# Cross-attention kernel: input tiles turned by VectorE's block transposition instead of TensorE, with layer norm statistics gathered through DRAM

## The chip, the cores and the metric

The kernel runs on one core of a Trainium2 chip (trn2). The metric is the device time of one execution in microseconds (us). Runs of the unchanged kernel lie between 3229.87 and 3229.97 us, with a median of 3229.92 us.

## The reference, cut to what matters

```python
# x: (32, 512, 512) queries, ctx: (32, 512, 512) keys and values; 16 heads of 32
def layer_norm(x, gamma, beta, eps=1e-05):
    mu = jnp.mean(x, axis=-1, keepdims=True)
    var = jnp.var(x, axis=-1, keepdims=True)
    return (x - mu) * jax.lax.rsqrt(var + eps) * gamma + beta

qn = layer_norm(q, q_norm_g, q_norm_b)
kvn = layer_norm(kv, kv_norm_g, kv_norm_b)
Q = (qn @ Wq).reshape(B, N_q, NUM_HEADS, D_HEAD).transpose(0, 2, 1, 3)
K = (kvn @ Wk).reshape(B, N_kv, NUM_HEADS, D_HEAD).transpose(0, 2, 1, 3)
V = (kvn @ Wv).reshape(B, N_kv, NUM_HEADS, D_HEAD).transpose(0, 2, 1, 3)
scores = jnp.einsum('bhqd,bhkd->bhqk', Q, K) / jnp.sqrt(jnp.float32(D_HEAD))
attn = jax.nn.softmax(scores, axis=-1)
ctx = jnp.einsum('bhqk,bhkd->bhqd', attn, V)
ctx = ctx.transpose(0, 2, 1, 3).reshape(B, N_q, D_ATTN)
out = q + jax.nn.gelu(ctx @ Wo + bo, approximate=False)
```

Everything is float32. The kernel splits each factor of a product into a high and a low part and adds three products of them.

## The kernel before, in words

The kernel goes through 32 batches. A batch has 512 query tokens and 512 context tokens of 512 features, held as eight tiles of 128 tokens (`tok`, tiles 0 to 3 from x and 4 to 7 from the context). The attention of a batch has four units of four heads; the loop body `batch(b)` has four steps, one for each unit.

The instruction streams of the five engines are written out by hand in the table `ORDER`: a string for each engine and step, whose words are the items of work, in the order in which the engine issues them (`s*4` is four items `s`). `items` turns the strings into a plan, and the code of each engine is one loop over its plan with an `if` for each kind. Each engine waits only through semaphores. What the items are:

- PE (TensorE): `st` is one matmul of transposed scores (L888), 16 in a step, which ACT turns into exponentials. `s` is one matmul of scores (L896), 16 in a step, from which DVE takes a maximum; it is for the unit of the next step. `st` and `s` share four PSUM banks in rotation. `q`, `k`, `v` and `o` are sixths of a projection, two matmuls each (L868). `pv` is one half of the product with V (L916), `z` the sums of rows (L859), `m` turns the maxima (L978; it ends a step). `x` turns one input tile: four transposing matmuls of 128x128 (L956).
- ACT (ScalarE): `st` the exponential (L575), `norm` applies the layer norm to a tile in place (L596), `x` takes the high part of a turned tile out of PSUM (L600), `mh` and `mx` write the maxima into `q_stack` (L625, L629), `gelu` (L592), and `q`, `k`, `v`, `split` copies.
- DVE (VectorE): `s` the maximum over a bank (L718), `ln` the statistics of a tile (`bn_stats`, L737), `la` their aggregation (`bn_aggr`, L743), `lv` variance plus epsilon and negated mean (L748, L749), `x` the low part of a turned tile (L694), `zt`, `zr`, `zb`, `cn` the normalization of the output (L723 to L734), `md` and `ml` for the maxima (L777, L783), `ob` the bias.
- POOL (GpSimd): `add` (L487), `ln` the power -1/2 and the negated shift of one tile (L503, L506), `res_add`, `split`.
- SP (SyncE) issues DMAs, all into one queue and in the order of its string: `load` an input tile (L398), `rq` and `rk` three DMAs each that restack the rows of q and k for the scores (L357), `rz` zero rows (L422), `store` and `res` the output and the residual (L441, L406). `rq`, `rk` and `rz` of a step serve the `s` items of the next one.

The projections, `v`, `o` and the turned tiles `x` share three PSUM banks `gen`. Their rotation is worked out from the order of PE's plan (`GEN`, `GEN_AT`, L161 to L171): before it writes a bank, an engine waits until the item three places back in the list has been taken out.

The input tiles of batch b+1 are loaded in step 0 of batch b, measured, normalized and turned in steps 0 and 1. Batch -1 is the head: it does this for batch 0, while the four weight matrices are loaded into `probs`, scaled and split.

The profile calls a stage here what lies between two `m` of PE. A batch is the stages of steps 3, 0, 1 and 2.

## Time and profile before

| what | value |
|---|---|
| median of the runs | 3229.92 us |
| the profiled execution | 3231.49 us |
| its span, first to last instruction | 3229.7 us |
| mean granted clock of TensorE | 0.997 of full speed |
| PE busy | 3196.3 us |
| POOL busy | 2318.6 us |
| ACT busy | 2306.6 us |
| DVE busy | 2274.2 us |
| DMA moved | 376.85 MB, 193,010 packets |

The page says of each engine how long it was busy. A matmul's record lasts longer than the time until the next one may start, so PE's own work is read from the chain of waits, where each piece counts until the next begins. The views by stage give each engine's busy time in a stretch that the reader chooses.

### The profile page before, as it was taken

What the parts mean: (1) busy time and instruction counts of PE and PEld (TensorE: products, weight loads), DVE (VectorE), ACT (ScalarE), POOL (GpSimd) and SP (SyncE); (2) the same over time, 40 slices, a digit from 0 to 9 for tenths busy, and PEclk for the clock granted to TensorE, in tenths of its full rate; (3) what the DMA queues carried; (4) which work ended last, traced back from release to release, by engine and by line L of the source; (5) the groups of instructions that cost most, each with busy time, mean ns of one, the idle gap of its engine ahead of it and who ended that gap; (6) DMA issues with size and microseconds to landing.
All of it is one profiled execution on the core that took longest, in us unless ns stands there. A gap on an engine that the chain in (4) does not pass through costs nothing.

```text
span 3229.7 us, 50112 instructions
## 1 busy us (share of the span) xinstructions
PE 3196.3 (99%) x16611; PEld 2148.0 (67%) x16611; DVE 2274.2 (70%) x4769; ACT 2306.6 (71%) x3985; POOL 2318.6 (72%) x1544
## 2 busy tenths in 40 slices
PE   8999999999999999999999999999999999999998
PEld 5566666666666666666666666666666666666664
DVE  6677677677677776776776777766767767777664
ACT  4677767777767777677777677776777776777765
POOL 2677677777777777777777777777777777777775
PEclk9999999999999999999999999999999999999999
DMA  4445445345444354453454444544534544544442
GB/s 147 101 104 129 115 119 133 95 115 137 115 115 120 104 130 115 120 133 95 115 136 116 115 119 105 130 115 121 131 95 115 138 115 114 121 105 128 115 102 79
DMA packets 193010, 376.85 MB, mean 117 GB/s; under 512 B 22625, under 2 KB 22641, under 8 KB 188658
## 3 DMA queue, kind: packets, MB, share of 16 engines
q1 hardware_dynamic: 192288, 372.86, 45.2%
q8 instruction: 134, 2.20, 0.3%
q14 instruction: 122, 1.00, 0.1%
q10 hardware_dynamic: 466, 0.80, 0.1%
HBM read 138.42 MB, written 33.82 MB: 53 GB/s over the span
## 4 chain that ended last, share of the span: by engine, by line
PE 98%; DVE 1%; ACT 1%; issue 0%; DMA 0%; ACTq 0%; POOL 0%
PE gen L868 43%; PE score L896 15%; PE score L888 15%; PE ctx L916 15%; PE gen L859 4%; PE gen L956 3%; PE gen L978 1%; DVE maxes L718 1%; PE score L800 0%; ACT probs L575 0%; PE gen L849 0%; ACT q_stack L629 0%; PE score L849 0%; ACT tok L596 0%; PE score L827 0%
## 5 line engine op out<-in xcount | busy, mean ns | idle before, releaser
L487 POOL TENSOR_TENSOR probs<-probs 128x1024 f32<-128x1024 f32 x762 | 1806.5, 2405 | 430.1 <-PE ctx L916 426.2
L718 DVE TENSOR_REDUCE maxes<-score 128x1 f32<-128x512 f32 x2048 | 1304.0, 681 | 267.8 <-PE score L896 256.7
L575 ACT ACTIVATE probs<-score 128x512 f32<-128x512 f32 x2048 | 1083.5, 606 | 229.7 <-PE score L888 219.9
L896 PE MATMUL score<-k_stack,q_stack 128*128 128x512 f32 x2048 | 728.7, 404 | 0.8 <-DVE maxes L718 0.2
L888 PE MATMUL score<-q_stack,k_stack 128*128 128x512 f32 x2048 | 713.9, 401 | 6.4 <-ACT q_stack L629 5.1
L896 PEld LDWEIGHTS score<-k_stack,q_stack 128*128 128x128 f32 x2048 | 380.0, 188 | 216.2 <-issue 81.1
L888 PEld LDWEIGHTS score<-q_stack,k_stack 128*128 128x128 f32 x2048 | 377.8, 188 | 185.6 <-ACT probs L575 42.4
L916 PE MATMUL ctx<-probs,v_sb 128*32 128x512 f32 x4096 | 492.4, 598 | 0.6 <-ACT probs L575 0.5
L868 PE MATMUL gen<-cT,w_k 128*128 128x512 f32 x1536 | 451.9, 399 | 0.1
L868 PE MATMUL gen<-xT,w_q 128*128 128x512 f32 x1536 | 444.0, 395 | 0.0
L868 PE MATMUL gen<-w_v,cT 128*128 128x512 f32 x1536 | 443.8, 390 | 0.0
L868 PE MATMUL gen<-w_o,ctx_hl 128*128 128x512 f32 x1488 | 401.5, 394 | 0.0
L503 POOL TENSOR_TENSOR rstd<-var_eps,minus_half 128x1 f32<-128x1 f32 x256 | 142.1, 555 | 322.5 <-DVE neg_mean L749 322.5
L696 DVE SCALAR_TENSOR_TENSOR k_nat<-gen,bias_k,k_nat 128x512 fp32r<-128x512 f32 x128 | 95.8, 749 | 357.9 <-ACT k_nat L620 357.9
L629 ACT ACTIVATE q_stack<-max_hl,chunk_mask 32x512 fp32r<-32x512 f32 x512 | 326.3, 706 | 29.7 <-DVE max_hl L783 28.2
L868 PEld LDWEIGHTS gen<-cT,w_k 128*128 128x128 f32 x1536 | 283.4, 191 | 80.1 <-DVE q_nat L696 27.0
L868 PEld LDWEIGHTS gen<-w_v,cT 128*128 128x128 f32 x1536 | 288.8, 188 | 62.6 <-issue 0.8
L868 PEld LDWEIGHTS gen<-xT,w_q 128*128 128x128 f32 x1536 | 288.7, 190 | 59.0
L868 PEld LDWEIGHTS gen<-w_o,ctx_hl 128*128 128x128 f32 x1488 | 274.9, 188 | 56.7
L916 PEld LDWEIGHTS ctx<-probs,v_sb 128*32 128x32 f32 x4096 | 109.3, 109 | 230.6 <-issue 206.8
L514 POOL TENSOR_TENSOR ctx_hl<-ctx_n,ctx_hl 128x512 fp32r<-128x512 f32 x128 | 164.9, 1288 | 99.8 <-ACT ctx_hl L581 99.7
L586 ACT ACTIVATE v_sb<-gen 128x512 f32<-128x512 f32 x128 | 76.1, 594 | 220.7 <-PE gen L868 220.7
(89 smaller groups left out, 2720.9 us busy)
## 6 DMA issues: line engine op xcount, KB each, us to landing
k_stack<-k_nat SPq DMA_DIRECT2D x384, 256.0 KB, 4.2
q_stack<-q_nat SPq DMA_DIRECT2D x381, 256.0 KB, 5.1
tok<-in_x SPq DMA_DIRECT2D x132, 256.0 KB, 6.0
tok<-in_ctx SPq DMA_DIRECT2D x128, 256.0 KB, 6.3
q_stack<-zero_rows SPq DMA_DIRECT2D x128, 256.0 KB, 3.3
res<-in_x SPq DMA_DIRECT2D x124, 256.0 KB, 2.6
out<-res SPq DMA_DIRECT2D x124, 256.0 KB, 2.5
probs<-in_L_xattn_Wq SPq DMA_DIRECT2D x1, 1024.0 KB, 8.5
```

Source lines behind the costliest of these rows:

```text
L487: pool.tensor_tensor(probs[:, c + 1, heads], probs[:, c + 1, heads], probs[:, c, heads], ALU.add).then_inc(pool_added, 1)
L503: pool.tensor_tensor(rstd[:, n:n + 1], var_eps[:, n:n + 1], minus_half[:], ALU.pow).then_inc(ln_rstd, 1)
L514: pool.tensor_tensor(ctx_hl[:, 1, up], ctx_n[:], raw(ctx_hl[:, 0, up]), ALU.subtract).then_inc(ctx_split, 1)
L575: act.activation(probs[:, n, part, :], score_at(s, "st", i)[:], ACT.Exp, scale=SCALE).then_inc(exp_done, 1)
L629: act.activation(q_stack[SROW:P, u1 % 2, :, P * n:P * (n + 1)], raw(max_hl[SROW:P, :]).unsqueeze(1).to_broadcast([SHIFTS, HU, P]), ACT.Ide ...
L718: dve.tensor_reduce(maxes[:, u1 % 2, SROW + i:SROW + i + 1], score_at(s, "s", i)[:], AX_X, ALU.max, negate=True).then_inc(max_done, 1)
L859: mm = pe.matmul(bank[DH * j:DH * (j + 1), :], ones[:, 0:DH], probs[:, c, j, :], start=(i == 0), stop=(i == len(chunks) - 1))
L868: mm = pe.matmul(bank[:, :], stationary(hs, c), moving(hm, c), start=(i == 0), stop=(i == len(TERMS) * NC - 1))
L888: pe.matmul(score_bank(pe, b, s, "st", i)[:, :], k_stack[:, s % 2, part, P * n:P * (n + 1)], q_stack[:, s % 2, part, :], start=True, stop= ...
L896: pe.matmul(score_bank(pe, b, s, "s", i)[:, :], q_stack[:, u1 % 2, n, P * part:P * (part + 1)], k_stack[:, u1 % 2, n, :], start=True, stop ...
L916: mm = pe.matmul(ctx_ps[DH * j:DH * (j + 1), :], v_sb[:, c, lo:lo + DH], probs[:, c, j, :], start=(c == 0), stop=(c == NC - 1))
L956: mm = pe.matmul(bank[:, P * c:P * (c + 1)], tok[:, n, P * c:P * (c + 1)], ident[:], start=True, stop=True, is_transpose=True)
```

## The change

The transposition of an input tile leaves PE. A tile `tok[:, n, :]` no longer holds 128 tokens with all their features. Partition 32g+j holds, of token 32t+j, the 128 features of group g, for eight values of t in a half of four groups by 1024 numbers. Its 32x32 blocks can then be turned in place by one DVE instruction (`xt`), which writes the whole bank that PE wrote before. The rows of the weights and the norm's gain and shift are loaded in the matching order. With it go:

- A load is a quarter of a pair of tiles: 16 DMAs of 128 KB for a batch, in pieces of 512 bytes, where there were 8 of 256 KB in pieces of 2 KB.
- `ln` makes four `bn_stats` of 128 columns for a tile, each of a quarter of a token's features. The four quarters lie on four groups of partitions. For two tiles at a time SP stores the statistics to DRAM (`gs`, one DMA of 24 KB) and loads them back to each of the four groups of partitions (`gl`, four DMAs of 24 KB). `la` aggregates them, four `bn_aggr` each, and `lv` and POOL's `ln` treat eight columns at once, four times a batch instead of eight.
- `norm` treats 128 columns, since scale and shift differ by group: 32 a batch instead of 8.
- `xt` is new on DVE, 8 a batch (L797 of the changed kernel). PE's `x` stays in its string only as the place in the rotation of the banks.
- All strings of `ORDER` are new; `items` lets loads and norm work begin in step 3 (a batch -2 is put ahead for it), which the strings of these kinds don't use.
- `ident` and `ones` now lie in `maxes`, `norm_rows` in `ctx_n`.

```diff
@@ ORDER: one line of PE's and SP's strings
-        "q*3 v*2 s q s q s v st*2 v st q st s st v st*2 v s v*2 st s st z s st*2 v st v*2 s*2 v st s pv st s "
-        "st s k st s*2 o s*2 pv m k*5 o*3",
+        "q s*2 q*2 st*2 q s st*2 q s st s q st*3 z st*2 v st s v st v st s st s v s*3 v*2 pv k st s k st k "
+        "s*4 pv k o m k*2 o*5",
...
-        "load*6 rz rq load*2 rk store res",
-        "rz rq rk",
+        "load*9 gs load*2 gl load gs load*2 gl load*2 gs rq gl rz rk store",
+        "gs gl rz rq rk res store",
...
+        x_turn = x.rearrange("b (t j) (g e) -> b g j t e", j=DH, e=P)
+        c_turn = ctx_in.rearrange("b (t j) (g e) -> b g j t e", j=DH, e=P)
...
-                    for n, (name, w) in enumerate((("q", wq), ("k", wk), ("v", wv), ("o", wo))):
-                        sp.dma_start(probs[:, n], w.rearrange("(c p) n -> p c n", p=P)).then_inc(w_loaded[name], 16)
...
-            def load_tile(b, i):
+            def load_weights(n, name, w):
+
+                turned = w.rearrange("(g c r) n -> g r c n", c=NC, r=DH)
+                for g in range(NG):
+                    sp.dma_start(probs[DH * g:DH * (g + 1), n], turned[g]).then_inc(w_loaded[name], 16)
+
+            def store_stats(b, k):
+
+                if known(b) and b == 0 and k % 2 == 0:
+                    load_weights(k // 2, "qk"[k // 2], (wq, wk)[k // 2])
+                wait(sp, ln_stats, 8 * b + 2 * (k + 1))
+                wait(sp, stats_spread, 64 * (4 * b + k))
+                sp.dma_start(stats_dram, stats[:, NH * k:NH * (k + 1), :].rearrange("p t s -> p (t s)")
+                             ).then_inc(stats_stored, 16)
+
+            def spread_stats(b, k):
+
+                wait(sp, stats_stored, 16 * (4 * b + k + 1))
+                wait(sp, ln_aggr, 8 * b + 2 * k)
+                for g in range(NG):
+                    sp.dma_start(stats_all[DH * g:DH * (g + 1)].rearrange("p g t s -> p g (t s)"),
+                                 stats_dram.rearrange("(g j) s -> j g s", j=DH)).then_inc(stats_spread, 16)
+
+            def load_half(b, h, g):
 
                 if valid(b - 1):
-                    wait(sp, full["x"], 8 * (b - 1) + i + 1)
-                src = x_v[NC * b + i] if i < NC else c_v[NC * b + i - NC]
-                sp.dma_start(tok[:, i, :], src).then_inc(tile_loaded[i], 16)
+                    wait(sp, full["x"], 8 * (b - 1) + 2 * (h + 1))
+                src = (x_turn if h < 2 else c_turn)[b, g, :, NH * (h % 2):NH * (h % 2 + 1), :]
+                sp.dma_start(tok[DH * g:DH * (g + 1), 2 * h:2 * (h + 1), :].rearrange("p i (t e) -> p (i t) e", e=P),
+                             src).then_inc(half_loaded[h], 16)
...
-                        if kind == "norm" and valid(b + 1):
-                            tile = tok[:, n, :]
-                            wait(act, ln_shift, 8 * (b + 1) + n + 1)
+                        if kind == "norm" and valid(bl):
+                            tile = tok[:, n // NG, P * (n % NG):P * (n % NG + 1)]
+                            wait(act, ln_shift, 4 * bl + n // NH + 1)
...
-                            dve.bn_stats(stats[:, n, :], tok[:, n, :]).then_inc(ln_stats, 1)
+                            for t in range(NG):
+                                op = dve.bn_stats(stats[:, NG * n + t, :], tok[:, n, P * t:P * (t + 1)])
+                            op.then_inc(ln_stats, 1)
...
-                            dve.bn_aggr(moments[:, n, :], stats[:, n, :]).then_inc(ln_aggr, 1)
+                            for t in range(NG):
+                                op = dve.bn_aggr(moments[:, NG * (n % 4) + t, :], stats_all[:, :, NG * (n % 2) + t, :])
+                            op.then_inc(ln_aggr, 1)
...
+                        if kind == "xt" and valid(b + 1):
+                            bank = gen_bank(dve, b, "x", n)
+                            wait(dve, ln_done, 2 * NT * (b + 1) + NG * (n + 1))
+                            dve.transpose(bank[:].rearrange("p (c t j) -> p c t j", c=NC, j=DH),
+                                          tok[:, n, :].rearrange("p (t c r) -> p c t r", t=NG, r=DH)).then_inc(full["x"], 1)
...
                         if kind == "x" and valid(b + 1):
-                            bank = gen_bank(pe, b, "x", n)
-                            wait(pe, ln_done, 8 * (b + 1) + n + 1)
-                            for c in range(NC):
-                                mm = pe.matmul(bank[:, P * c:P * (c + 1)],
-                                               tok[:, n, P * c:P * (c + 1)], ident[:], start=True,
-                                               stop=True, is_transpose=True)
-                            mm.then_inc(full["x"], 1)
```

The rows below are of the program's order, not of its times. The first place is SP's queue in step 0, where the last input tiles are loaded and q and k are restacked. Before:

```order
L398 DMA tok<-in_x 128x512 x4
L398 DMA tok<-in_ctx 128x512 x2
L422 DMA q_stack<-zero_rows 32x2048
L357 DMA q_stack<-q_nat 32x4x512 x3
L398 DMA tok<-in_ctx 128x512 x2
L357 DMA k_stack<-k_nat 32x4x512 x3
L441 DMA out<-res 128x512
```

Now, from the twelfth load on:

```order
L426 DMA tok<-in_ctx 32x8x128
L410 DMA stats_dram<-stats 128x48
L426 DMA tok<-in_ctx 32x8x128 x2
L418 DMA stats_all<-stats_dram 32x4x48 x4
L426 DMA tok<-in_ctx 32x8x128 x2
L410 DMA stats_dram<-stats 128x48
L361 DMA q_stack<-q_nat 32x4x512 x3
L418 DMA stats_all<-stats_dram 32x4x48 x4
L456 DMA q_stack<-zero_rows 32x2048
L361 DMA k_stack<-k_nat 32x4x512 x3
```

The restack of q now stands behind three stores and two reloads of statistics, and that of k behind a third reload, all of which wait for something.

The second place is DVE's queue in the middle of step 1, where the tiles of x are turned. Before (`tok` to `gen` is done by PE):

```order
L694 TENSOR_TENSOR xT<-gen,xT 128x4x128
L718 TENSOR_REDUCE maxes<-score 128x1
L748 TENSOR_SCALAR var_eps<-moments 128x1
L749 TENSOR_SCALAR neg_mean<-moments 128x1
L718 TENSOR_REDUCE maxes<-score 128x1
L734 TENSOR_TENSOR ctx_n<-ctx,ctx_n 128x512
```

Now:

```order
L756 TENSOR_REDUCE maxes<-score 128x1
L782 MEMSET spare 128x1
L784 BN_AGGR moments<-stats_all 128x2 x4
L797 STREAM_TRANSPOSE gen<-tok 128x512
L734 SCALAR_TENSOR_TENSOR k_nat<-gen,bias_k,k_nat 128x512
L782 MEMSET spare 128x1
L784 BN_AGGR moments<-stats_all 128x2 x4
L732 TENSOR_TENSOR xT<-gen,xT 128x4x128
L756 TENSOR_REDUCE maxes<-score 128x1
L797 STREAM_TRANSPOSE gen<-tok 128x512
```

Between two maxima now stand up to seven other items, among them the transpositions that PE made.

The third place is ACT's queue at the end of step 1, ahead of the maxima (`max_cut`). Before:

```order
L596 ACTIVATE tok<-tok,neg_shift,rstd 128x512 x3
L600 ACTIVATE cT<-gen 128x4x128 x3
L592 ACT_TABLE_LOAD
L592 ACTIVATE act_out<-gen 128x512
L625 ACTIVATE max_cut<-gen,cut_sign 32x128
```

Now:

```order
L632 ACTIVATE tok<-tok,neg_shift,rstd 128x128 x3
L639 ACTIVATE xT<-gen 128x4x128
L632 ACTIVATE tok<-tok,neg_shift,rstd 128x128 x2
L639 ACTIVATE xT<-gen 128x4x128
L632 ACTIVATE tok<-tok,neg_shift,rstd 128x128 x6
L627 ACT_TABLE_LOAD
L627 ACTIVATE act_out<-gen 128x512
L632 ACTIVATE tok<-tok,neg_shift,rstd 128x128 x3
L664 ACTIVATE max_cut<-gen,cut_sign 32x128
```

The norms have become many short instructions, and the high parts of the context tiles have moved into step 2.

## Rows read from the trace of the kernel before

**Rows 1.** Page, part 1: busy time, share of the span and instructions

```profile
PE 3196.3 (99%) x16611; PEld 2148.0 (67%) x16611; DVE 2274.2 (70%) x4769; ACT 2306.6 (71%) x3985; POOL 2318.6 (72%) x1544
```

**Rows 2.** Chain that ended last, one batch: shares by line, pieces (start, us, what)

```profile
by line: PE gen L868 44.7%; PE score L896 15.9%; PE score L888 15.7%; PE ctx L916 15.1%; PE gen L859 4.0%; PE gen L956 3.6%; PE gen L978 1.2%; issue 0.0%
...
1476.42 0.47 PE gen L956 x4
...
1480.84 0.23 PE score L896
```

**Rows 3.** Windows, stages of steps 0, 1, 2, 3: span, busy (instructions), PEclk, DMA, GB/s

```profile
1445.13:1466.99 21.86, 21.86 (x114) 14.38 (x115) 16.51 (x41) 15.07 (x27) 17.06 (x14) 1.00 0.25 85
1466.99:1499.97 32.98, 32.98 (x180) 23.86 (x180) 25.00 (x58) 26.62 (x43) 26.44 (x21) 1.00 0.63 152
1499.97:1519.84 19.87, 19.87 (x107) 12.62 (x106) 14.55 (x26) 16.11 (x28) 11.13 (x7) 1.00 0.05 14
1421.27:1445.13 23.86, 23.85 (x121) 15.80 (x122) 14.34 (x25) 13.92 (x26) 18.02 (x10) 1.00 0.79 189
```

**Rows 4.** Groups by line, whole span: busy us, mean ns of one, idle before

```profile
L743 DVE BATCH_NORM_AGGREGATE moments<-stats 128x2 f32<-128x6 f32 x256 | 45.0, 176 | 0.0
L643 DVE TENSOR_REDUCE head_mask<-ident 128x4 f32<-128x128 f32 x1 | 0.3, 276 | 0.0
L723 DVE STREAM_TRANSPOSE ctx_n<-gen 128x512 f32<-128x512 f32 x128 | 91.7, 716 | 107.9 <-PE gen L859 105.8
L625 ACT ACTIVATE max_cut<-gen,cut_sign 32x128 fp32r<-32x128 f32 x128 | 46.0, 359 | 257.6 <-PE gen L978 257.6
L629 ACT ACTIVATE q_stack<-max_hl,chunk_mask 32x512 fp32r<-32x512 f32 x512 | 326.3, 706 | 29.7 <-DVE max_hl L783 28.2
L596 ACT ACTIVATE tok<-tok,neg_shift,rstd 128x512 f32<-128x512 f32 x256 | 197.5, 810 | 6.3 <-POOL neg_shift L506 5.5
```

**Rows 5.** Timeline of DVE, that batch: start, us, what

```profile
1436.15 8.63 DVE L718 TENSOR_REDUCE maxes<-score 128x1 f32<-128x512 f32 x14
...
1448.78 0.69 DVE L737 BATCH_NORM_STATS2 stats<-tok 128x6 f32<-128x512 f32 x1
1449.39 1.27 DVE L718 TENSOR_REDUCE maxes<-score 128x1 f32<-128x512 f32 x2
...
1474.02 0.18 DVE L743 BATCH_NORM_AGGREGATE moments<-stats 128x2 f32<-128x6 f32 x1
...
1474.11 0.12 DVE L748 TENSOR_SCALAR var_eps<-moments 128x1 f32<-128x1 f32 x1
```

**Rows 6.** Timeline of ACT, that batch: start, us, what

```profile
1474.29 1.28 ACT L592 ACT_TABLE_LOAD   x1
...
1488.44 2.22 ACT L596 ACTIVATE tok<-tok,neg_shift,rstd 128x512 f32<-128x512 f32 x3
```

**Rows 7.** Timeline of SP's DMA issues, that batch: start, us, what

```profile
1472.59 2.24 SPq L357 DMA_DIRECT2D k_stack<-k_nat  x3
1484.23 0.35 SPq L441 DMA_DIRECT2D out<-res  x1
1486.28 0.33 SPq L406 DMA_DIRECT2D res<-in_x  x1
```

**Rows 8.** Page, part 6: DMA issues, KB each, median us from issue to landing

```profile
k_stack<-k_nat SPq DMA_DIRECT2D x384, 256.0 KB, 4.2
q_stack<-q_nat SPq DMA_DIRECT2D x381, 256.0 KB, 5.1
...
tok<-in_ctx SPq DMA_DIRECT2D x128, 256.0 KB, 6.3
```

**Rows 9.** The head: a DMA in the chain, first product with w_k on PE

```profile
1.95 3.09 DMA norm_rows<-in_L_xattn_kv_norm_b
...
32.51 3.01 PE L868 MATMUL gen<-cT,w_k 128*128 128x512 f32 x12
```

162 lines of the change are left out of this document (86 added, 76 removed), and 25 rows, old and new, of the table ORDER.

## The prediction

> **What bounds the kernel now.** I read the busy shares first. PE is busy for 99% of the span, the three others for 70 to 72% [rows 1]. That a matmul's record is longer than its place in the queue makes "busy" weak evidence, so the next view is the chain of waits over one batch in the middle, from 1421.53 to 1520.10 us, which is 98.57 us. It is PE from end to end: the lines of PE make up 100% of it and issue 0.0% [rows 2]. The four stages of that batch say the same: PE is busy for 98.56 of 98.57 us, at the full granted clock, and never waits [rows 3]. So any time taken from PE is gained, as long as nobody then comes late, and any wait given to PE is lost. The stages also show who has room. DVE is busy for 16.5 of 21.9 us in step 0, 25.0 of 33.0 in step 1, 14.6 of 19.9 in step 2 and 14.3 of 23.9 in step 3; ACT for 15.1, 26.6, 16.1 and 13.9 us [rows 3].
>
> **What goes.** The line L956 has 3.6% of 98.57 us, which is 3.55 us a batch, or 0.44 us for each of eight tiles; a piece of four matmuls in the chain has 0.47 us [rows 2]. All of it is on the path. The tiles of batches 1 to 31 are turned inside full batches, so 31 x 3.55 = 110 us go. The batch without waits would take 98.57 - 3.55 = 95.0 us.
>
> **How long the new stages are.** PE's times come from the chain's shares [rows 2]: a sixth of a projection 0.46 us (44.7% of 98.57 over 96 of them), a score matmul 0.24 us (31.6% over 128), half a pv 1.86, z 0.99, m 0.30. The new string of step 1 has 23 sixths and 32 scores: 10.6 + 7.8 + 3.7 + 1.0 + 0.3 = 23.4 us. Likewise step 0 comes to 23.8 us (24 sixths), step 2 to 21.5 (19) and step 3 to 26.5 (30). In step 1 before, 33.0 us were there for much of the same side work.
>
> **DVE.** Prices are from start to start of the next instruction. Fourteen maxima take 8.63 us, which is 0.61 each [rows 5]; a tile's `bn_stats` has the same 0.61 [rows 5]. No row shows one of 128 columns. At least a quarter, 0.15; at most 0.28, the reduction of 128x128 on this engine [rows 4]. I take 0.20: 384 columns less at the rate of 512 in about 0.55 us. Four make 0.8 us instead of 0.61, so eight `ln` cost 1.5 us more a batch. `bn_aggr` starts its follower after 0.09 us with its memset included [rows 5] and lasts 0.18 [rows 4]. With four groups instead of one to merge I take 0.12, between these two; `la` becomes 0.5 us instead of 0.1, eight cost 3.2 more (bounds 2.2 to 5). `xt` streams 512 columns as the maxima do: between their 0.61 and the 0.72 of L723 [rows 4, 5] I take 0.65, so 5.2 us for eight. `lv` saves some 0.4. DVE's batch goes from 70.4 us (the sum of its stages [rows 3]) to 80, of 95.
>
> The average is not the limit, the stage is. By the new strings, with the prices above, 0.6 to 0.75 for other full-width instructions, step 1 gives DVE 16.7 us of old items and 6.5 of new ones (four `xt` 2.6, four `la` 2.0, two `ln` 1.6, two `lv` 0.3), together 23.2 us in a stage of 23.4. Since the first `s` can only run when k is restacked, 6 us into the stage, DVE cannot spread this evenly: from the first maximum to the last it has 17.3 us of work (15 maxima 9.2, the rest 8.1), while PE issues the same scores in 15.9. Four banks hold at most four scores, and `m` waits for the last maximum. So PE ends step 1 about 1.4 us late, 1.6 with the moment in which DVE starts behind. In step 0 the two `la` and an `ln` stand between maxima 7 and 9, while PE issues four scores in 1 us and then half a pv. Walked in order, PE is held there by about 0.5 us. Step 2 has 19.9 of 21.5 us for DVE and recovers; step 3 has 13.7 of 26.5. For DVE I count 2.1 us a batch. At the low prices (0.15, 0.09, 0.61) it is about 0.6, at the high ones (0.28, 0.18, 0.72) about 4.
>
> **ACT.** A norm of 512 columns costs (2.22 - 0.81) / 2 = 0.70 us from start to start [rows 4, 6]. No row has one of 128 columns, but two neighbours differ in little but their columns: 128 last 0.36 us (L625), 512 last 0.71 (L629) [rows 4]. So 384 columns are worth 0.35, and the short norm costs 0.70 - 0.35 = 0.35 us, within 0.18 (a quarter) and 0.46 (0.81 - 0.35, its whole duration). Thirty-two make 11.2 us instead of 5.6. Step 1 has 20 of them, 16 exponentials, six `x`, four gelu and three loads of a table at 1.28 us [rows 6]: 29 us in a stage of 23.4. The surplus of about 6 us runs into step 2, which has 16.4 of 21.5. PE is held where the first exponentials of step 2 are due, and I count 0.4 us a batch (0 to 1.5). The Trainium skill, in "VectorE: DVE Perf Modes", section "The TRN2 errata", says that small instructions pay a fixed cost each and gives ScalarE 224 cycles plus the columns at 1.2 GHz, which would make the short norm 0.29 us and the 32 of them 2 us cheaper than by the rows. By its formula the long norm would be 0.61, and the trace has 0.70, so the rows are not replaced by it.
>
> **POOL** gets four power instructions of eight columns for eight of one, ahead of nothing urgent: zero.
>
> **SP and its queue.** This is the added wait. In step 0 the queue now goes store, reload, store, reload, store, then q's restack, a third reload, zero rows, k's restack, and each store waits for the reload before it. Say R for a store until it can be reloaded and S for a reload. R is 1486.28 - 1484.23 = 2.05 us, the issue of a residual that waits for an output store [rows 7], so 2.3 with loads ahead of it in the queue. S is four issues and a landing. The smallest DMA of the trace, one of 2 KB, took 3.09 us beside others [rows 9]; a 256 KB restack lands in 4.2 [rows 8]. I take 4. The second `ln` ends some 5.6 us into step 0, so k's restack can start at 5.6 + 3R + 2S + 2 = 22.5 us, and its work on DVE is finished at about the same time. Before, its first issue came 1480.84 - 1472.59 = 8.25 us ahead of the first score that needs it [rows 2, 7], with three issues in 2.24 and the last landing 4.2 later, 1.8 to spare. Now that score stands at 30.3 us: 7.8 us. It just holds, so I count zero. With R = 3 and S = 5 (the loads of the trace land in 6.3 behind one another [rows 8]) it is 4.1 us later, and 2 to 3 of these are lost. The Trainium skill, in "DMA: Bandwidth & Descriptors", section "Anatomy of one DMA — SWDGE (gpsimd) path", gives about 2.0 us of fixed cost for a transfer (measured on another issuing path than SP's). By it alone R would be 2.0 and S about 3.5, and 3 us would be to spare. The trace's 3.09 for 2 KB is above it.
>
> **The head.** Before, PE's first product with w_k starts at 32.5 us [rows 9]. Now four pairs of store and reload stand one behind the other, with the four weight matrices (4 MB) between them: 4 x (2.3 + 4) is 25 us, after some 6 for the first load and statistics, plus about 10 for the weights and the last norms: 41. I count 8 us more (2 to 15). The tail does not change.
>
> **Sum.** 3231.5 - 31 x (3.55 - 2.1 - 0.4) + 8 = 3231.5 - 32.6 + 8 = 3207. The profiled execution is 1.6 us above the median, so 3205.
>
> **Rivals.**
> *The strings hold.* DVE's and ACT's new instructions cost what the low bounds say and PE waits 0.3 us a batch: 3230 - 31 x 3.25 + 6 = 3135. For it speaks that PE has no wait at all before, in spite of equally tight strings; against it, that step 1 is overfull by the middle prices already.
> *The round trips through DRAM decide (slower).* The mechanism has one place: k's restack in step 0 behind the third reload, and the `la` between the maxima behind the first. It decides as soon as 3R + 2S passes 16.3 us (the forecast has 14.9, and k's restack 1.4 to spare). With R = 3 and S = 5 the batch takes 2.5 us more for k and 1 for `la`, on top of the forecast: 3205 + 31 x 3.2 = 3304. For it speaks that DMA is already the busy side in steps 3 and 1 (share 0.79 and 0.63 [rows 3]), against it, that steps 0 and 2 have 0.25 and 0.05.
> *The bank stays.* PE loses its transposition but its place in the rotation of three banks remains, now held for DVE's `xt`, ACT's copy and DVE's subtraction, two of which queue behind maxima. If the products behind wait 0.3 us for each of eight tiles, 2.4 us a batch come in the place of half of the other losses (1.25): 3205 + 31 x 1.15 = 3241.
>
> **How the numbers follow.** Forecast 0.42, strings hold 0.24, round trips 0.24, bank 0.10. The forecast's own range is 3165 to 3250. The whole range is 3132 to 3312. A change of 2% is 64.6 us and about what a measurement of this kernel can tell from none: 3165.3 and 3294.5. Faster: nine tenths of the second case and a little of the first, 0.24. Slower: about two thirds of the third and a little of the bank, 0.19. The rest, 0.57, is within 2%.
>
> **What would show it.** In the changed profile PE should have no L956, and small idle times before L888 and L896 with the maxima of DVE as their releaser, in step 1 above all. `bn_stats` should start their followers after 0.20, the short norms after 0.35. If PE's largest wait is for a DMA of `k_stack`, or DVE's for `stats_all`, the round trips have it. If PE shows no waits, the batch is 95 us and the forecast is too slow. It is wrong in its head if the first product with w_k starts before 35 or after 48 us.

## The result and the profile after

The changed kernel takes 3423.43 us (3414.78 to 3432.07 in two runs) against 3229.92 us. The ratio is 1.0599, with a 95% interval of 1.0484 to 1.0714. It is slower by 6%, and lies above the whole predicted range. All the rows below are from its slower execution, of 3432.07 us, whose span is 3430.3 us. The two runs are 17 us apart, so a difference of 10 us to this kernel says nothing.

The page, parts 1 and 4, answers to [rows 1] and [rows 2]:

```profile
PE 3210.5 (94%) x15587; PEld 2047.4 (60%) x15587; DVE 2644.1 (77%) x6304; ACT 2555.6 (75%) x4753; POOL 2357.5 (69%) x1288
...
PE 66%; DVE 10%; issue 7%; POOL 6%; DMA 4%; SPq 3%; ACT 3%; POOLq 0%; DVEq 0%; ACTq 0%
```

TensorE lost 1024 matmuls, and the chain that was TensorE alone now has a third of its length elsewhere. The stages of steps 0, 1, 2 and 3 of one batch, with the columns of [rows 3]:

```profile
1653.42:1677.18 23.76, 23.58 (x120) 15.43 (x120) 19.38 (x63) 18.33 (x35) 17.98 (x11) 1.00 0.47 103
1677.18:1709.22 32.04, 28.94 (x135) 18.79 (x133) 27.59 (x77) 27.17 (x51) 23.45 (x15) 0.95 0.57 132
1709.22:1733.86 24.64, 22.58 (x112) 13.87 (x112) 20.93 (x35) 20.57 (x39) 16.95 (x10) 1.00 0.16 54
1733.86:1757.89 24.03, 24.02 (x125) 15.90 (x122) 13.99 (x25) 13.59 (x25) 15.54 (x8) 1.00 0.73 169
```

I read the period of a batch as the median distance of `m` to the `m` four stages on, in the trace of each kernel. It was 98.62 us and is 103.94. The first `m` of TensorE came at 62.61 us and comes at 98.47; from the first to the last it is 3131.1 us before and 3295.5 now. So the 200 us between the two profiled executions are 36 of the head and 164 of 31 batches (5.3 each).

To see which stage lost, count what TensorE issues from one `m` to the next at the prices of the prediction (0.46 for a sixth of a projection, 0.24 for a score, 1.86 for half a `pv`, 0.99 for `z`, 0.3 for `m`). Packed without waits, the stages of steps 0 to 3 would be 23.4, 26.6, 21.5 and 23.8 us, together 95.2. Their medians over the run are 23.75, 31.02, 24.66 and 24.05. Steps 0 and 3 are within 0.4 us of that; step 1 is 4.4 us over and step 2 3.2.

Who TensorE waits for, between 150 and 3300 us (total, times, longest). In the same view of before the only row is 0.2 us of issue:

```profile
PE gen L916 <- DVE k_nat L734: 45.0, 23, 2.0
PE gen L1019 <- DVE maxes L825: 34.7, 29, 2.2
PE gen L916 <- DVE cT L732: 23.8, 30, 0.8
PE score L936 <- ACT q_stack L668: 23.6, 31, 2.8
PE gen L907 <- POOL probs L521: 8.5, 34, 0.4
PE score L944 <- DVE maxes L756: 7.9, 15, 0.7
```

The largest wait is for the low part of k early in step 1, and nothing of the prediction stands there. (This view lists idle times above 0.15 us; shorter ones are in no list of this document.) Here is one, on VectorE, TensorE and POOL (timeline: start, us, what):

```profile
1679.04 0.41 DVE L791 TENSOR_SCALAR var_eps<-moments 128x8 f32<-128x8 f32 x1
1679.37 2.41 DVE L792 TENSOR_SCALAR neg_mean<-moments 128x8 f32<-128x8 f32 x1
1681.81 0.75 DVE L734 SCALAR_TENSOR_TENSOR k_nat<-gen,bias_k,k_nat 128x512 fp32r<-128x512 f32 x1
```

```profile
1682.61 2.66 PE L916 MATMUL gen<-xT,w_q 128*128 128x512 f32 x6 [1.96 <-DVE k_nat L734]
...
1687.76 1.09 PE L916 MATMUL gen<-cT,w_k 128*128 128x512 f32 x4
```

The stretch of these six matmuls, in the columns of [rows 3]:

```profile
1682.61:1685.27 2.66, 2.66 (x7) 2.12 (x8) 2.66 (x12) 0.96 (x2) 2.66 (x2) 0.57 0.69 206
```

```profile
1672.31 14.08 POOL L521 TENSOR_TENSOR probs<-probs 128x1024 f32<-128x1024 f32 x6
```

A `tensor_scalar` of eight columns takes 2.41 us while POOL is inside a row of additions; k is behind it on VectorE, and TensorE idles for 1.96 us. After that idle time six matmuls take 2.66 us, where four a little later take 1.09. The granted clock of these 2.66 us is 0.57 of full speed, so most of them ran at the lower of TensorE's two levels (1.2 and 2.4 GHz); the whole stage has 0.95, the three others 1.00.

The clock is a part of the loss of its own. Of the 32 stages of step 1, 12 have a granted clock under 0.97, and their median is 32.0 us where the other 20 have 30.4. Of the 32 of step 2 it is 11, with 25.75 against 24.64 us. The kernel before has one such stage in either step.

The groups of the new and changed operations (busy us, mean ns of one, idle before):

```profile
L777 DVE BATCH_NORM_STATS2 stats<-tok 128x6 f32<-128x128 f32 x1024 | 218.8, 276 | 2.0 <-DMA tok<-in_x 0.7 <-DMA tok<-in_ctx 0.4
L797 DVE STREAM_TRANSPOSE gen<-tok 128x512 f32<-128x512 f32 x256 | 181.4, 709 | 35.5 <-ACT act_out L627 32.6 <-ACT tok L632 2.7
L784 DVE BATCH_NORM_AGGREGATE moments<-stats_all 128x2 f32<-128x24 f32 x1024 | 155.5, 219 | 27.5 <-issue 27.0
...
L792 DVE TENSOR_SCALAR neg_mean<-moments 128x8 f32<-128x8 f32 x128 | 85.9, 671 | 0.0
L791 DVE TENSOR_SCALAR var_eps<-moments 128x8 f32<-128x8 f32 x128 | 33.6, 263 | 2.3
```

```profile
L632 ACT ACTIVATE tok<-tok,neg_shift,rstd 128x128 f32<-128x128 f32 x1024 | 440.6, 487 | 32.6 <-POOL neg_shift L541 31.8
...
L539 POOL TENSOR_TENSOR rstd<-var_eps,minus_half 128x8 f32<-128x8 f32 x128 | 211.3, 1651 | 111.8 <-DVE neg_mean L792 111.8
```

### The profile page after: what moved, and what is told of

The parts are those of the page before. It is cut to its first block, busy times and chain, and to the rows that moved or that the text cites. A ratio compares the mean times of both kernels' runs of the same rounds, so it can differ in the third digit from the quotient of the medians.

```text
span 3430.3 us, 51274 instructions
## 1 busy us (share of the span) xinstructions
PE 3210.5 (94%) x15587; PEld 2047.4 (60%) x15587; DVE 2644.1 (77%) x6304; ACT 2555.6 (75%) x4753; POOL 2357.5 (69%) x1288
## 4 chain that ended last, share of the span: by engine, by line
PE 66%; DVE 10%; issue 7%; POOL 6%; DMA 4%; SPq 3%; ACT 3%; POOLq 0%; DVEq 0%; ACTq 0%
PE gen L916 27%; PE score L936 13%; PE score L944 10%; PE ctx L964 10%; POOL probs L521 5%; PE gen L907 4%; DMA res<-in_x 4%; DVE maxes L756 3%; SPq L361 2%; DVE neg_mean L792 2%; POOL res L546 1%; DVE moments L784 1%; DVE gen L797 1%; DVE k_nat L734 1%; ACT q_stack L668 1%
## 5 line engine op out<-in xcount | busy, mean ns | idle before, releaser
L610 ACT ACTIVATE probs<-score 128x512 f32<-128x512 f32 x2048 | 1119.5, 610 | 232.3 <-PE score L936 209.7
L936 PE MATMUL score<-q_stack,k_stack 128*128 128x512 f32 x2048 | 748.4, 415 | 28.4 <-ACT q_stack L668 27.0
L916 PE MATMUL gen<-xT,w_q 128*128 128x512 f32 x1536 | 477.7, 416 | 73.2 <-DVE k_nat L734 49.4
L632 ACT ACTIVATE tok<-tok,neg_shift,rstd 128x128 f32<-128x128 f32 x1024 | 440.6, 487 | 32.6 <-POOL neg_shift L541 31.8
L916 PE MATMUL gen<-w_o,ctx_hl 128*128 128x512 f32 x1488 | 416.7, 398 | 0.7
L916 PEld LDWEIGHTS gen<-xT,w_q 128*128 128x128 f32 x1536 | 300.6, 199 | 162.4 <-DVE k_nat L734 62.0
L539 POOL TENSOR_TENSOR rstd<-var_eps,minus_half 128x8 f32<-128x8 f32 x128 | 211.3, 1651 | 111.8 <-DVE neg_mean L792 111.8
L664 ACT ACTIVATE max_cut<-gen,cut_sign 32x128 fp32r<-32x128 f32 x128 | 46.0, 360 | 289.8 <-PE gen L1019 289.0
```

Of the source, the lines that this page charges most:

```text
L539: pool.tensor_tensor(rstd[:, of], var_eps[:, of], minus_half[:], ALU.pow).then_inc(ln_rstd, 1)
L610: act.activation(probs[:, n, part, :], score_at(s, "st", i)[:], ACT.Exp, scale=SCALE).then_inc(exp_done, 1)
L632: act.activation(tile, tile, ACT.Identity, bias=neg_shift[:, n:n + 1], scale=rstd[:, n:n + 1]).then_inc(ln_done, 1)
L916: mm = pe.matmul(bank[:, :], stationary(hs, c), moving(hm, c), start=(i == 0), stop=(i == len(TERMS) * NC - 1))
L936: pe.matmul(score_bank(pe, b, s, "st", i)[:, :], k_stack[:, s % 2, part, P * n:P * (n + 1)], q_stack[:, s % 2, part, :], start=True, stop= ...
```

## The experiments

Sixteen kernels were run besides before and after. The table gives their times, the ratio to before of the same chip, the period of a batch, its stages of steps 0, 1, 2, 3 (medians, us) and the first `m`. Before, after and e1 to e4 had two timed runs each, the others four (e12 ten). Kernels marked * leave part of the computation out. A median hides that two kinds of batches take turns in after, e2 and e4 (clock full or not), so the length from the first to the last `m` is given where it says something else.

| kernel | us | ratio (95%) | batch | stages | first m |
|---|---|---|---|---|---|
| before | 3229.92 | 1 | 98.62 | 21.8, 32.9, 20.0, 23.9 | 62.6 |
| after | 3423.43 | 1.060 (1.048-1.071) | 103.94 | 23.8, 31.0, 24.7, 24.1 | 98.5 |
| e1 | 3378.51 | 1.045 (1.042-1.048) | 102.09 | 23.8, 29.5, 24.7, 24.1 | 98.2 |
| e2* | 3420.66 | 1.058 (1.048-1.069) | 103.71 | 23.8, 31.9, 24.0, 24.1 | 98.2 |
| e3* | 3343.55 | 1.035 (1.032-1.038) | 101.25 | 23.8, 29.4, 24.0, 24.0 | 95.1 |
| e4* | 3376.93 | 1.045 (1.038-1.052) | 102.87 | 23.8, 29.9, 24.7, 24.0 | 76.9 |
| e5* | 3313.20 | 1.024 (1.023-1.026) | 100.73 | 23.8, 28.9, 24.0, 24.1 | 77.6 |
| e6* | 3326.65 | 1.029 (1.027-1.030) | 100.41 | 23.5, 28.7, 24.0, 24.1 | 98.6 |
| e7* | 3355.24 | 1.038 (1.036-1.039) | 101.32 | 23.8, 29.2, 24.1, 24.1 | 95.0 |
| e9 | 4046.03 | 1.251 (1.249-1.253) | 123.63 | 33.5, 30.1, 24.8, 35.2 | 94.6 |
| e10* | 3297.20 | 1.020 (1.018-1.021) | 100.22 | 23.6, 28.6, 24.0, 24.1 | 67.9 |
| e11* | 3269.84 | 1.012 (1.010-1.013) | 99.53 | 23.6, 28.5, 23.4, 24.0 | 67.2 |
| e12 | 3230.80 | 0.999 (0.998-1.000) | 98.65 | 21.8, 32.9, 20.0, 23.9 | 61.3 |
| e13 | 3411.24 | 1.055 (1.054-1.057) | 103.31 | 23.8, 29.4, 25.9, 24.1 | 97.1 |
| e14 | 3387.62 | 1.048 (1.047-1.050) | 102.12 | 23.7, 29.6, 24.6, 24.0 | 98.8 |
| e15* | 3304.78 | 1.022 (1.021-1.024) | 100.40 | 23.6, 28.8, 24.0, 24.1 | 66.9 |
| e16* | 3200.10 | 0.990 (0.989-0.992) | 97.52 | 21.8, 31.8, 20.0, 24.0 | 62.1 |
| e17 | 3357.93 | 1.039 (1.037-1.040) | 102.13 | 23.8, 29.5, 24.7, 24.1 | 78.9 |

### The long tensor_scalar, and the power: e1, e2, e3

```diff
# e1: lv without tensor_scalar; EPS stands in a third column of moments
-dve.tensor_scalar(var_eps[:, of], mom[:, :, 1], EPS, None, ALU.add)
-dve.tensor_scalar(neg_mean[:, of], mom[:, :, 0], -1.0, None, ALU.mult)
+dve.tensor_reduce(var_eps[:, of], mom[:, :, 1:3], AX_X, ALU.add)
+dve.tensor_reduce(neg_mean[:, of], mom[:, :, 0:1], AX_X, ALU.add, negate=True)
# e2: POOL multiplies by -0.5 where it raised to the power; e3: both
-pool.tensor_tensor(rstd[:, of], var_eps[:, of], minus_half[:], ALU.pow)
+pool.tensor_tensor(rstd[:, of], var_eps[:, of], minus_half[:], ALU.mult)
```

> Edit: variance plus epsilon and negated mean are made by two tensor_reduce of 8 columns (epsilon lies in a third column of moments) instead of two tensor_scalar of 8 columns. Theory 'port': one of the two tensor_scalar lasts up to 2.4 us instead of 0.16 because it waits until GpSimd's running add of 2.4 us lets go of SBUF; in step 0 it stands ahead of k's low part, so TensorE misses a bank, pauses and comes back at the lower clock. Then no such instruction lasts over 0.4 us here, TensorE's wait for k_nat (49 us in all) goes, and the time falls by 60 to 125 us, to 3300 to 3360. Theory 'round trips' (statistics through DRAM set the pace) and theory 'GpSimd' (its power of 8 columns lasts 1.65 us): the time stays within 15 us of the changed kernel.

> Edit: GpSimd's power of 8 columns becomes a multiplication of the same columns (the power -1/2 of the variance is left out of the layer norm). Theory 'GpSimd': in step 1 GpSimd runs without a gap from the first pv to z of step 2, so 4 x 1.4 us less work frees at least the one that stands among the adds: z comes 1.4 to 2 us earlier in a batch and the time falls by 40 to 80 us. Theory 'port': GpSimd's work does not bound, the lock stays, and the time falls by under 20 us. Theory 'round trips': no change.

> Edit: both of the former (the power is left out). If port and GpSimd are two separate losses, the gains add: 100 to 200 us less than the changed kernel, 3220 to 3320. If what remains is the density of DVE's and ACT's short instructions as forecast (2.5 us a batch) and a longer head, the time is near 3260. If the round trips bound behind them, it is not under 3330.

In e1 the same two numbers per column come from `tensor_reduce`, and both stay short. Its groups:

```profile
L792 DVE TENSOR_REDUCE var_eps<-moments 128x8 f32<-128x16 f32 x128 | 20.6, 161 | 2.3
L793 DVE TENSOR_REDUCE neg_mean<-moments 128x8 f32<-128x8 f32 x128 | 19.5, 152 | 0.0
```

The wait for `k_nat` is gone from TensorE's list, one stage of step 1 in 32 has a granted clock under 0.97 where 12 had, step 1 is 1.5 us shorter, and 45 us go by the medians (1.85 a batch, 52 us in all, by the two profiled executions). That is less than the 60 to 125 us that the theory gave. In e2 POOL's instruction falls from 1651 to 206 ns, but with the long `tensor_scalar` still there it gives nothing that the two runs resolve: step 2 is 0.7 us shorter, and TensorE waits 76.6 us for `k_nat` (150 to 3150 us) in the place of 43.1. On top of e1 the same edit gives 35 us, 0.84 a batch, most of it in step 2. Together the two edits take 80 us, less than the 100 to 200 expected, and at 3343.55 us the time lies where the text on e3 put the third theory (not under 3330); e5 below tests that one.

Why the power costs time in step 2 can be read from ScalarE. Its norms wait for POOL, and the copies of the maxima into `q_stack` stand behind norms. In e1 `max_cut` starts 0.88 us after `m` and the first transposed score 5.25; in e3 it is 0.34 and 4.60 (medians). TensorE's wait for `q_stack`, of e1 and then of e3, 150 to 3150 us:

```profile
PE score L937 <- ACT q_stack L668: 24.5, 29, 3.5
PE score L937 <- ACT q_stack L668: 7.8, 22, 2.7
```

With it the lower clock goes from step 2: 10 of 32 stages in e1, 2 in e3.

### Is it the shape? e12, on the kernel before

```diff
...
+    if n % 2:
+        dve.tensor_scalar(wide_out[:, 0, :], wide_in[:, :, 1], EPS, None, ALU.add)
+        dve.tensor_scalar(wide_out[:, 1, :], wide_in[:, :, 0], -1.0, None, ALU.mult)
```

> The kernel before with two tensor_scalar of 8 columns added behind every second lv, from and to tiles that nothing else uses (8 a batch). Theory that a tensor_scalar of 8 columns, unlike one of 1 column, shares something with POOL and waits for the end of its instruction: their longest lasts over 2000 ns where one met a running add, the 1-column ones in the same places stay below 250 ns, and the time rises by 0 to 30 us (8 short instructions at 0.1 us are 0.8 us of DVE a batch, hidden where no wait comes). Rival, that the long ones in the changed kernel wait for something of that kernel (moments or the semaphore before them): all 8-column instructions stay at 150 to 250 ns, and the time is within 5 us of before.

The groups of e12, new rows (128x8) and its own (128x1), and the spread of one new line (min/median/max):

```profile
L755 DVE TENSOR_SCALAR wide_out<-wide_in 128x8 f32<-128x8 f32 x128 | 78.6, 614 | 0.0
L752 DVE TENSOR_SCALAR neg_mean<-moments 128x1 f32<-128x1 f32 x256 | 36.3, 142 | 0.0
```

```profile
L756 DVE TENSOR_SCALAR wide_out<-wide_in x128: 155/164/2441, 8.4 to 3065.0; 128x8 f32<-128x8 f32 x128
```

The theory holds: the eight-column form in a kernel that had no such wait lasts up to 2.4 us and 614 ns on average, the one-column form beside it 142, and never over 153. It costs this kernel nothing (0.9992, 0.9983 to 1.0002), since nothing urgent is behind it there. The length of the wait is that of POOL's instruction. All 32 eight-column ones over 300 ns in e12, and all 67 in after, end within 0.25 us of the end of an instruction on POOL, and none that starts while POOL is idle lasts over 172 ns.

### The exchange through DRAM: e4, e5

```diff
-sp.dma_start(stats_dram, stats[:, NH * k:NH * (k + 1), :]...)
-for g in range(NG): sp.dma_start(stats_all[DH * g:DH * (g + 1)]..., stats_dram...)
-bn_aggr(moments[...], stats_all[:, :, NG * (n % 2) + t, :])
+bn_aggr(moments[...], stats[:, NG * n:NG * (n + 1), :])
```

> Edit: the statistics' stores and reloads are left out; bn_aggr takes the 24 numbers of its own partition (so mean and variance are those of a group of features of four tokens, which the reference does not have). Theory 'round trips': the time falls by 80 us or more. Theory 'port' and 'GpSimd': in full batches nothing changes by this; only the head, in which four pairs of store and reload stand in a row, gets 15 to 25 us shorter, so the time falls by 15 to 40 us.

> Starts from e3 (3343.6 us) and leaves out the store and the reload of the statistics as well; each partition aggregates its own 24 numbers, so that the means and variances are not those of whole tokens. Theory that the round trips hold step 1 through k's late restack: with the lock and the powers gone, the chain of e3 in step 1 still starts at the landing of k_stack and is bound by DVE only from there. Then step 1 falls from 29.4 us by about 1 (to 28.5 or less) and the head's first m comes from 95 to about 74 us, in all 21 + 31 x 1 = 52 us less, about 3292 us. Rival, DVE's density in step 1: k's restack comes sooner but DVE is still late at the last maximum; only the head's 21 us go, about 3322 us, with step 1 within 0.3 us of 29.4. Should the whole rest of the loss be the round trips, the time would fall to 3231 - 110 + 36 - 21, about 3150 us.

Without the exchange (alone in e4, on top of e3 in e5) the head is 21.5 and 17.5 us shorter, and a batch 1.07 and 0.52. Between the first and the last `m` that is 24 and 14 us; the intervals of e4 and after overlap, so e4's figure for a batch rests on its trace alone. In e5 neither pure theory holds: step 1 falls by 0.5, TensorE's wait for `k_stack` from 13.6 to 1.4 us, and TensorE still waits at the end of the step. So the exchange is the larger part of the head's 36 us and a small one of a batch.

### The new work of VectorE and ScalarE: e6, e7, e10, e11

```diff
# e6: one bn_stats and one bn_aggr for each item in the place of four
# e7: one norm of 512 columns in the place of four of 128
# e10: e5, e6 and e7 together
# e11: e10, and xt, the high and the low part treat 128 of 512 columns
+cut = NC if known(b) and b < 1 else 1
```

> Starts from e3 (3343.6 us); DVE makes one bn_stats and one bn_aggr for each item where it made four, so three quarters of the statistics are left out, in every step, and everything else is issued as before. By the durations in the changed kernel (276 ns and 219 ns, start to start 0.2 and 0.16) this takes 3 x 0.2 x 8 + 3 x 0.16 x 8 = 8.6 us a batch from DVE, of them about 3 in step 1. Theory that DVE's density in step 1 is what is left of the loss in e3: step 1 falls from 29.4 to about 27 us and a batch from 101.2 to 98 or 99, about 3343 - 31 x 2.7 = 3260 us. Rival, ACT's short norms (they delay the copies of maxima and the first exponentials of step 2): step 1 changes by less than 0.7 us and step 2 stays at 24.0; above 3315 us.

> Starts from e3 (3343.6 us); ACT makes one norm of 512 columns for each tile in the place of four of 128, with one group's scale and shift for all four, so the normalized numbers are those of another token for three quarters of a tile. By 0.385 us a short norm and 0.70 a long one this takes 8 x (4 x 0.385 - 0.70) = 6.7 us a batch from ACT, of them 3 to 4 in step 1 and 1 in step 2. Theory that ACT's surplus of step 1 runs into step 2: step 2 falls from 24.0 to about 22 us, step 1 by less than 1, about 3343 - 31 x 2.5 = 3266 us. Rival, DVE's density alone: step 2 stays above 23.5 us and the time above 3320 us.

> Everything new but the transposition made light at once: e3 (3343.6 us) without the store and reload of statistics, with one bn_stats and one bn_aggr for each item in the place of four, and with one norm of 512 columns for four of 128. Left out are the rest of the statistics, the exchange, the power and three quarters of the scales. In the trace of e3 TensorE's waits of step 1 are 1.26 us a batch for the last maximum, 0.5 for k_stack and 0.4 for exponentials, in step 2 0.92 for the low part of a context tile (cT) and about 1.6 for score banks, and each of e5, e6 and e7 alone gave 0 to 0.8 us a batch. Theory of many near ties (each edit alone only uncovers the next): a batch of 97.5 us or less, 3215 us or less with the head at 15 us above before. Rival, that the transposed tiles themselves (the chain xt, high part, low part through one bank) and the order around them hold PE: a batch of 99 us or more, 3260 us or more, with the wait for cT still at 0.9 us a batch.

> Starts from e10; from batch 1 on the chain of a turned tile is made short: DVE's transposition, ACT's high part and DVE's low part treat 128 of 512 columns each (three quarters of every tile keep old values), in the same places of the strings. That takes 16 x 0.4 = 6.4 us a batch from DVE and about 2.8 from ACT. Theory that this chain is what holds PE in steps 1 and 2: the waits for the last maximum in step 1 (about 1 us) and for cT in step 2 (0.9 us) both fall below 0.3 us, a batch 1.5 to 2.5 us below e10, 45 to 80 us. Rival, that the order of PE's own string holds it (first st of step 2 too soon after m): less than 20 us below e10.

e6 takes 7 us of busy time a batch from VectorE and gains 0.84; e7 takes 6.3 from ScalarE and gains nothing, it is even 12 us slower than e3. Both of my theories about them failed in size.

But e7 is not a clean cut of ScalarE's work. The one long norm of a tile stands in the place of its fourth short one, and in step 1 that place is between the maxima and their copies (timeline of ACT in e7, `m` at 1063.8 us):

```profile
1064.29 0.36 ACT L666 ACTIVATE max_cut<-gen,cut_sign 32x128 fp32r<-32x128 f32 x1 [2.11 <-PE gen L1022]
1064.68 0.81 ACT L634 ACTIVATE tok<-tok,neg_shift,rstd 128x512 f32<-128x512 f32 x1
1065.52 1.33 ACT L670 ACTIVATE q_stack<-max_hl,chunk_mask 32x512 fp32r<-32x512 f32 x2
```

A short norm of 0.49 us stood there. So the first transposed score comes 5.08 us after `m` (4.60 in e3), TensorE waits 22.0 us for `q_stack` (7.8 in e3), and 9 stages of step 2 have a low clock (2 in e3). What ScalarE's 32 short norms cost is not shown by e7, and e10, e11 and e15 carry the same long norm.

All together (e10) the batch is 100.22 us, only 1.0 below e3. That is the rival's side, and its other mark is there too:

```profile
PE gen L1014 <- DVE maxes L820: 25.4, 30, 0.9
PE gen L911 <- DVE cT L729: 23.7, 30, 0.8
PE score L931 <- ACT q_stack L662: 16.8, 27, 1.0
```

With the chain of the turned tiles cut short (e11) the wait for `cT` goes and a batch is 0.69 shorter, less than forecast (27 us, for 45 to 80); the wait for the last maximum does not move at all:

```profile
PE gen L1016 <- DVE maxes L822: 25.4, 30, 0.9
PE score L933 <- ACT q_stack L663: 15.7, 29, 1.0
PE gen L904 <- POOL probs L513: 15.0, 46, 0.5
```

Its cause has changed, though. In the last 8 us before the `m` of step 1 VectorE is idle for 0.03 or 0.04 us in after, e1 and e10. In e11 it is idle for 1.17: the bias `ob` stands in its queue ahead of the last five maxima and waits for a sixth of o. From e11's list of VectorE's waits:

```profile
DVE gen L804 <- PE gen L913: 45.9, 75, 1.2
```

### Other places for the work: e9, e13, e14, e15

```diff
# e9: e1, loads and six ln in step 3, most la, lv, norm in step 0; DVE's step 3:
-"k zt s zr zb cn s*2 q s*13 md ml"
+"k ln*4 zt s zr zb s*2 cn q s*5 la*2 lv s*4 ln*2 s*4 md ml"
# e13: e1, DVE's step 2 and ACT's end of step 1
-"ob s xt s xt ob x ..."    "... norm*3 mh norm mx*2 gelu mx*2 x split x gelu"
+"ob s xt s xt x ob ..."    "... norm*3 mh mx*4 gelu x norm split x gelu"
# e14: e1, PE's and DVE's end of step 1 (e15: the same on e10)
-"s*2 o s*2 pv o s*2 o s o*2 s o*2 m"    "... s xt s x s ob s*5 md x ml"
+"s*2 o s*3 pv o s*2 o s o*4 m"          "... s xt s x s*2 ob s*4 md x ml"
```

> The changed kernel's computation in full, with the lock out of it (both columns that POOL reads are made by tensor_reduce) and another order: loads and the first six of eight statistics of the next batch in step 3, the reloads and the rest in step 3 and step 0, most norms in step 0, so that step 1 loses two thirds of its short norms, its two ln and its four la. Theory that the loss is one of placement (three engines full in step 1, not in step 3): step 1 falls to 27.5 us or less, step 2 to 23 or less, and a batch to 96 to 98.5 us, 3180 to 3260 us in all (the head is not made shorter). Rival, that the new work costs the same wherever it stands: a batch at 101 us or more, above 3330 us.

> The computation in full: e1 (3378.5 us, no tensor_scalar in lv) with two places of the strings changed. DVE in step 2 makes the low part of the first context tile ahead of the bias (x ob for ob x), and ACT at the end of step 1 makes its four copies of maxima without a norm and a gelu between them (norm*3 mh mx*4 gelu x norm for norm*3 mh norm mx*2 gelu mx*2 x). Theory that PE's two waits at the start of step 2 are set by these places: the wait for cT falls from 0.93 to about 0.4 us and the first st comes about 0.9 us sooner, together 1.0 to 1.4 us a batch, about 3340 us. Rival, that the next thing is late at once (gelu's bank, exponentials behind the table load): within 12 us of 3378.

> The computation in full: e1 (3378.5 us) with one place of step 1 changed. TensorE issues one score more ahead of the second half of pv and has four sixths of o behind the last score in the place of two (o s*3 pv o s*2 o s o*4 m for o s*2 pv o s*2 o s o*2 s o*2 m); VectorE takes one maximum more ahead of its bias (s*2 ob s*4 for s ob s*5). In e11, whose VectorE has much less to do, TensorE still waited 1.0 us for the last maximum: five scores come in 2.1 us behind pv, their maxima and the bias last 3.7 us. Theory that this wait is made by the order of these two strings: it falls from 1.27 to 0.4 us a batch or less, step 1 by 0.7 to 1.0 us, the time by 22 to 31 us (about 3352 us). Rival, that VectorE's density makes it (it never is idle from the first maximum on): the last maximum ends no earlier, under 10 us.

> e10 (3297.2 us, all side work light) with the same change of the end of step 1 as e14. By the theory of order the wait for the last maximum goes from 1.0 us to below 0.3 us a batch: 3270 to 3276 us. By the rival (density) e10 would have had no such wait at all; with that already fallen, the other result would be that the next thing is late at once: under 8 us.

e9 was badly placed by me. VectorE's first `ln` stands at the start of step 3, where SP has only begun to issue the loads, and `la` stands too close behind it for its reload (there the profile names no releaser); everything behind them on VectorE waits (its own waits, 150 to 3900 us):

```profile
DVE moments L780 <- issue: 268.0, 30, 9.2
...
DVE stats L773 <- DMA tok<-in_x: 139.8, 50, 5.5
```

Step 1 lost its `ln`, `la`, `lv` and most norms and is still 30.1 us. That tells little about the theory, since TensorE's clock was low for a part of 31 of the 32 stages. One of them:

```profile
1620.52:1650.61 30.09, 29.24 (x134) 19.41 (x134) 20.32 (x35) 24.33 (x43) 13.20 (x8) 0.92 0.42 105
```

Whether the work would fit elsewhere stays open. e13 and e14 each move one wait to another place. In e13 the first transposed score no longer waits 24.5 us in all for `q_stack` (3.4), but 32.2 for a score bank that VectorE has not emptied, since it now stands behind the low part of a tile; the time rises by 33 us, where a fall of about 40 or a change within 12 was expected. A part of the rise is the clock, low in 17 stages of step 2 (10 in e1). In e14 the wait for the last maximum falls from 35.0 to 16.4 us, the time rises by 9 us, and scores now wait 18.4:

```profile
PE score L945 <- DVE maxes L757: 18.4, 32, 0.8
PE gen L1020 <- DVE maxes L826: 16.4, 30, 1.8
```

e15 says the same with light side work (14.5 and 8.8; 8 us slower than e10). So moving two scores only moves the wait. In e1 and e10 VectorE has no idle time ahead of that last maximum, which is the density that the rival of e14 named; in e11 it is the place of the bias. No run moves that bias in e11's kernel.

### The term of the gain by itself: e16, on the kernel before

```diff
-for c in range(NC):
+for c in range(NC if known(b) and b < 1 else 1):
     mm = pe.matmul(bank[:, P * c:P * (c + 1)], tok[:, n, P * c:P * (c + 1)], ident[:], ...)
```

> The kernel before with its transposition by TensorE cut to one matmul of four from batch 2 on (three quarters of a turned tile keep what is in the bank); strings, loads, statistics and norms are its own. This tests the term of the gain alone: 3/4 of 3.55 us are taken from TensorE in 30 batches, 80 us. Theory that time taken from TensorE is gained as long as the old strings hold: 3152 us, within 15. Rival, that with less work on TensorE the same maxima, exponentials and turned tiles come late (the strings of before were cut for its own length): less than half, above 3190 us, with waits for maxes, cT or probs on TensorE.

With everything else as before, 2.66 us less work for TensorE in a batch gives 1.1 (33 us of 80). All of the 1.6 us that are missing are lost in step 1 again. The list has one large wait there, for ScalarE's exponentials:

```profile
PE ctx L916 <- ACT probs L575: 13.9, 31, 0.5
```

That is 0.45 us a batch. Shorter waits are in no list, but the issue times of the two kernels can be laid side by side, item for item (medians of 29 batches). Half of the missing time stands ahead of the two halves of `pv` (0.74 us, exponentials), 0.35 us around a sixth of o whose bank was held for VectorE's low part of a tile, and the rest in pieces of 0.1 us.

### The head: e17

```diff
# e1, with w_q, w_k, w_v and w_o loaded behind the fourth reload of statistics
-if known(b) and b == 0 and k % 2 == 0:
-    load_weights(k // 2, "qk"[k // 2], (wq, wk)[k // 2])
```

> The computation in full: e1 (3378.5 us) with the head's DMAs in another order, nothing else: all four weight matrices are loaded behind the fourth reload of statistics, where w_q stood ahead of the first store, w_k ahead of the third and w_v and w_o ahead of the fourth. In the changed kernel the four stores of the head are issued at 7.0, 16.5, 22.7 and 32.9 us, each 5.5 to 7.3 us before its reload, where a store and its wait are taken as about 2 us when nothing is in front of them. Theory that the weights in the same queue make the head's round trips long: the first reload follows its store within 3.5 us, the fourth is issued by about 28 us in the place of 40, and the first m comes from 98.2 to 78 to 86 us, 3358 to 3366 us in all. Rival, that the round trips are as long without them or that the weights are then late themselves (4 MB behind 28 us): the first m above 92 us, within 8 us of 3378.

SP's issues in the head, first of after, then of e17:

```profile
7.02 0.43 SPq L410 DMA_DIRECT2D stats_dram<-stats  x1
...
13.19 1.74 SPq L418 DMA_DIRECT2D stats_all<-stats_dram  x4
...
32.90 0.38 SPq L410 DMA_DIRECT2D stats_dram<-stats  x1
40.15 1.74 SPq L418 DMA_DIRECT2D stats_all<-stats_dram  x4
```

```profile
6.87 0.35 SPq L406 DMA_DIRECT2D stats_dram<-stats  x1
...
8.36 1.75 SPq L414 DMA_DIRECT2D stats_all<-stats_dram  x4
...
21.92 0.34 SPq L406 DMA_DIRECT2D stats_dram<-stats  x1
23.40 1.74 SPq L414 DMA_DIRECT2D stats_all<-stats_dram  x4
```

A store of 24 KB can be reloaded after 1.5 us when no weights stand ahead of it, and after 6.2 and 7.25 when 1 to 2 MB do. The first product with w_k starts at 46.6 us in the place of 65.9 (e1), the first `m` comes 19 us sooner, and the whole is 20.6 us faster. It is the best version of the changed kernel that was run, and still 3.9% slower than before.

## Why the prediction was wrong, point by point

**"Any time taken from PE is gained, as long as nobody then comes late": this step failed first.** The line L956 was 3.55 us a batch and did go. But e16 takes three quarters of it from the old kernel, strings and all, and gets 41% of that. TensorE's 99% hid that ScalarE's exponentials, and after them a bank that VectorE empties, were next to it in step 1. At that rate, which is an estimate for the whole term, it was worth 1.5 us a batch.

**The stages' lengths were misread.** The 23.8, 23.4, 21.5 and 26.5 us count the items of each string. A stage goes from `m` to `m`, and seven sixths behind the `m` of step 0 and six behind that of step 3 run in the next one: 23.4, 26.6, 21.5 and 23.8 us. So "23.2 us in a stage of 23.4" for VectorE, and 29 for ScalarE, were set against a length 3 us too short. In the stage of step 1 shown above VectorE was busy for 27.6 us and ScalarE for 27.2.

**"`lv` saves some 0.4": wrong in sign, and the largest single cause.** I counted eight columns for one as the same instruction made half as often. It is 1.85 us a batch (e1; 1.6 by the length from the first to the last `m`), with the lower clock behind the wait in it. No rival named it. The Trainium skill has it, in "SBUF — State Buffer", section "Who interferes with whom": VectorE's `tensor_scalar` in its two-port mode and a GpSimd instruction exclude each other for a whole instruction, and a `tensor_reduce` never does. The Trainium skill, in "VectorE: DVE Perf Modes", section "Mode 2×_2P — use both read ports for one tensor", adds that source and destination must lie in SBUF and have an even number, or an odd and equal one, in their outermost dimension that is not one. By these rules a single column does not enter the mode and eight do. The runs agree: 614 and 142 ns in e12, 161 and 152 ns for `tensor_reduce` in e1. I had read the price of `lv` off rows of one column and not asked in which way eight differ.

**VectorE's prices were good.** Four `bn_stats` start their follower after about 0.8 us as said, `xt` after 0.63 (said 0.65), an item `la` of four `bn_aggr` after 0.55 to 0.74 (said 0.5). The mechanism at the end of step 1 was right as well: said was that PE comes 1.4 to 1.6 us late there, and e1 to e5 wait 1.1 us in the list, 1.3 with the gaps too short for it. "Step 2 recovers" was wrong. Step 2 is 3.2 us over its packed length.

**ScalarE: 0.4 us a batch was mis-sized, and its cause misplaced.** A short norm takes 0.385 us from start to start (said 0.35). Whether the number of norms costs anything is not shown: e7 puts four in one, but lengthens the one that the copies of the maxima stand behind. What is late is the chain behind `m`: copies of the maxima, gelu, high part of a context tile, low part. Between `m` and the first transposed score of step 2 TensorE had seven sixths and seven scores, 4.9 us; now it has seven sixths and three scores, 4.2 us, and waits for `q_stack` (0.76 us a batch in the list) and for `cT` (0.77). Two thirds of the wait for `q_stack` go with POOL's power (e3). e13 shows that the pieces of this chain can't be swapped freely.

**POOL "zero": wrong.** Eight columns of the power last 1651 ns, and one lasted 555 before:

```profile
L503 POOL TENSOR_TENSOR rstd<-var_eps,minus_half 128x1 f32<-128x1 f32 x256 | 142.1, 555 | 322.5 <-DVE neg_mean L749 322.5
```

Half as many instructions cost more in all (211.3 us busy for 142.1), and ScalarE's norms in front of the maxima wait for them, so they were not "ahead of nothing urgent". It is worth 0.84 us a batch once the long `tensor_scalar` is gone (e3 against e1).

**SP's chain "just holds, zero": short by 0.5 to 1.1 us a batch.** By SP's timeline R is 1.5 to 1.8 us in the batches (said 2.3). TensorE's wait for `k_stack` is 2.4 us in the whole run, but there it waits for `k_nat` first: it is 9.0 in e1 and 13.6 in e3. Taking the exchange out gives 1.07 or 0.52 us a batch (e4, e5).

**The head: 36 us for 8.** The first product with w_k starts at 66.1 us, where the prediction said 41 and called itself wrong in its head after 48:

```profile
66.13 3.04 PE L916 MATMUL gen<-cT,w_k 128*128 128x512 f32 x12
```

From there to the first `m` it is 32.3 us, 30.1 before, so nearly all of the 36 lie ahead of it. The form of the sum (four round trips in a row) was right, R in it was not: 5.5 to 7.3 us with weights in the same queue. "Plus about 10 for the weights" counted them once, where they stand ahead of three of the four stores. e17 gives 19 us back by the order alone.

**The rivals.** "The bank stays" named a real wait (`cT`, 0.77 us a batch in the list, gone in e11), at a third of its price. "Round trips decide" holds for part of the head. "The strings hold", with 0.3 us of waits a batch, has e16 against it: there the cut alone brings 1.6 us of waits. The sum of "round trips decide" was slipped: 2.5 and 1 us are 3.5 a batch, and 3.2 was put in, so its 3304 should be 3313.5.

**The sum as it should have stood,** a batch, from the runs: +1.85 the long `tensor_scalar`, +0.84 the power, +0.52 the exchange, +0.51 statistics and norms, +0.69 the chain of turned tiles, in the order in which they were taken out (103.94, 102.09, 101.25, 100.73, 100.22, 99.53). Between the first and the last `m` of the traces these are 52, 32, 14, 9 and 27 us of the 164, and 31 are left. The 99.53 that is left is above the old kernel's 98.62 with nearly all new work gone, and 4.3 over the packed 95.2. That part was not settled beyond this: e11's list shows the last maximum (0.8 us a batch), the copies of maxima (0.5) and POOL's additions (0.5), and e14 and e15 show that moving one wait raises another. The wait for the copies is at least in part made by e11's own long norm.

## What to carry to other kernels

Before you book time as gained on an engine that is busy for 99%, shorten its work alone in the old kernel and see how much arrives: here it was 41%, because other engines were next in the same stage. Count the lower clock behind a wait with the wait, and look at the granted clock of each stage before you say what an experiment shows (e9), and at what stands next to an instruction that an edit lengthens (e7). When an edit makes a small instruction wider, ask whether it changes how the instruction runs, not only how long: go by a row of the same form, and for VectorE beside a busy POOL take a form whose rows don't stretch (`tensor_reduce` here). And put small transfers that somebody waits for ahead of large ones in the same queue.

## What the runs showed of the hardware that I had not expected

- A `tensor_scalar` of 128x8 in SBUF lasts 152 to 2441 ns beside POOL's 2.4 us additions, and the long ones end with POOL's instruction; one of 128x1 lasts 142 ns on average and 153 at most (e12).
- POOL's power takes 555 ns for one column and 1651 for eight; a product of the same eight takes 206 (e2).
- After 1.96 us of idle time on TensorE the next six matmuls took 2.66 us, at a granted clock of 0.57: a short wait can cost more than its length. Waits for `q_stack` of 0.8 us a batch go with a low clock in 10 of the 32 stages of step 2 in e1, waits of 0.3 us with 2 in e3.
- A 24 KB store can be reloaded after 1.5 us with no weights ahead of it in its queue (e17), and after 7.25 us behind 2 MB of them (after).
